# One loop, seven trips of two batches in place of fourteen trips of one

## The chip, the cores and the metric

The kernel runs on one core of a Trainium2 chip. The core has five engines that run at once, each with an instruction stream of its own: TensorE (PE: matrix products and transposes), VectorE (DVE), ScalarE (ACT), GpSimd (POOL) and SyncE (SP, which here only issues DMAs). In front of each engine a sequencer reads the stream, works out register values, waits for semaphores, branches, and hands the real work to its engine. In the profile, a name with a q at its end (ACTq, DVEq, PEldq) is such a sequencer. The metric is the time of one execution on the device in microseconds (us), lower is better; three runs of the kernel before gave 1945.77, 1946.47 and 1946.70 us.

## The reference, cut to what matters

Each of 16 batches (512 tokens of width 256) goes through a normalisation, an attention branch of 16 heads with a feed-forward part, and a gated branch whose operands are rounded to a 4 bit grid; the two are multiplied and added to the input:

```python
x = L0_attn_x                                  # (16, 512, 256)
xn = _layernorm(x, axis=-1)
s = _L0_attn_ref(xn, ...)                      # attention, layernorm, gelu feed-forward, layernorm
g = _silu(_L0_ffn_ref(xn, w_gate, w_up, w_down))
x = x + s * g
```

## The kernel before, in words

All work is written out by hand as named steps, one ordered list for each engine (`ORDER`). There are three parts. The part `head` prepares weights and handles the first batch, the part `end` handles the last one, and the part `mid` is the steady state. One pass through `mid` is one batch, but it is a software pipeline: it takes the attention scores of batch b, the output side (`cT`, `out`, `hT`, `f1`, `f2`) of batch b-1 and the input side (`xT`, `proj`, `v`) of batch b+1.

The five engines meet only through semaphores that count up over the whole kernel and are never reset. `Event.wait` (L68) turns a batch number into the count to wait for: `b * (per * by) + (k + 1) * by`. Where b is known, that is a constant; in the loop b is a register, and the sequencer works the count out (ALU_OP and FUSED_REGOPS records of L68) just ahead of the instruction that waits for it.

`program` (L1630 to L1634) puts the parts together for one engine: the head once, then a loop of fourteen trips over `mid` with the trip's register as the batch number, then the end. Each engine has its own loop and its own branch back; there is no barrier at the end of a trip. At this seam the engines do the following, and the steps of the prediction are here:

- TensorE ends its list with `ctxt.3 mT.0 dn.3` (L716 is `dn`) and begins it with `cT` (L723: eight transposes of the finished attention context) and `out.0 out.1` (L731: the output projection).
- ScalarE ends with `mT.0 dn.3` (L812, L878) and begins with `cT` (L889: copies the transposed context to `catT`, which `out` reads).
- VectorE ends with `mfin.0 ctxt.3 dn.3` (L1125 is `dn`) and begins with `out.0 out.1` (L1133: adds the projection to `hY`), then `ln1`.
- SyncE ends with `fin mio.0` and begins with `T.0 load.1`: loads of the tables `Tz` (L552) and of `KS` and `QS` (L527).
- GpSimd ends with `hr.3` and begins with `ln1`, which waits for VectorE.

So in the order of the data the seam is: `dn.3` on TensorE, `cT` on TensorE, `cT` on ScalarE, `out` on TensorE, `out` on VectorE.

Of the kernel before, what the change touches and what calls it, by code (L numbers as in the profile page):

```python
# [15 lines left out]
B, S, D = 16, 512, 256  # L16
# [40 lines left out]
class Event:  # L57
# [5 lines left out]
    def wait(self, eng, b, k=None):  # L63

        if isinstance(b, int) and b < 0:
# [96 lines left out]
    mid=dict(  # L162
        sync="""
            T.0 load.1 T.1 T.2 xload T.3 mio.1 T.4 splitio T.5 load.0 T.6 T.7 fin mio.0
        """,
        gpsimd="""
            ln1 mul.0 lnb1 xnb mul.1 hq.0 mul.2 hr.0 projm.0 mul.3 hq.1 projm.1 hr.1 projm.2 xq xr mul.4 hq.2 mul.5
            ln2 hr.2 fin mul.6 hq.3 mul.7 hr.3
        """,
        vector="""  # L170
# [140 lines left out]
def build(nc, x_d, w, out_d):  # L311
    with ExitStack() as ctx:
# [1316 lines left out]

        def program(steps, eng):  # L1630
            steps(eng, "head", PARTS["head"])
            with eng.Fori(1, B - 1) as b:
                steps(eng, "mid", dict(mid=b))
            steps(eng, "end", PARTS["end"])  # L1634

        with nc.Block() as block:
            @block.sync
            def _(sp):
                program(sync_steps, sp)
                d_out.wait(sp, B - 1, 1)  # L1640

            @block.gpsimd
            def _(pool):
                program(gpsimd_steps, pool)

            @block.vector
            def _(dve):
                program(vector_steps, dve)

            @block.tensor  # L1650
            def _(pe):
                program(tensor_steps, pe)

            @block.scalar
            def _(act):
                program(scalar_steps, act)
# [33 lines left out]
```

How the kernel before makes its waits and increments, by code:

```python
    def wait(self, eng, b, k=None):  # L63
        if isinstance(b, int) and b < 0:
            return
        k = self.per - 1 if k is None else k
        eng.wait_ge(self.sem, b * (self.per * self.by) + (k + 1) * self.by)
# [350 lines left out]
        def inc(ins, name):  # L419
            ins.then_inc(E[name].sem, 1)
# [56 lines left out]
        def sync_steps(sp, part, at_batch):  # L477
# [27 lines left out]
                        cols, r = slice(t * P, (t + 1) * P), 2 * H * t  # L505
                        sp.dma_start(qb_d[:, 3:6, cols], bias_sp[r:r + H]).then_inc(d_split.sem, 16)
                        sp.dma_start(kb_d[:, 0:3, cols], bias_sp[r + H:r + 2 * H]).then_inc(d_split.sem, 16)
                elif k == "load":
                    half = s[1]
                    hb = half_batch(half, b)
                    if which != "pro":
                        E["pe_sc"].wait(sp, hb - 1, 24 * half + 23)
                    if which == "pro":
                        sp.wait_ge(L["ready"], 3)
                        sp.wait_ge(L["ones"], 32)
                    d_split.wait(sp, hb)
                    pairs = slice(HALF * half, HALF * (half + 1))
# [24 lines left out]
                        E["g_mul"].wait(sp, b, p - 2)  # L543
                    else:
                        v_mul[1].wait(sp, b - 1, PAIRS - 2 + p)
                        E["g_mul"].wait(sp, b - 1, PAIRS - 2 + p)
                    if which == "first" and p < 2:
                        sp.wait_ge(L["rows"], 16 * 5)
                    for e in range(2):
                        r = rows_d[b, 2 * p + e, :]
```

## Time and profile before

| | us |
|---|---|
| median of three runs (lowest to highest) | 1946.47 (1945.77 to 1946.70) |
| profiled execution, its time | 1947.52 |
| its span, first to last instruction | 1945.70 |
| TensorE busy (matrix products) | 1820.7 (94%) |
| VectorE busy | 1615.3 (83%) |
| GpSimd busy | 1103.7 (57%) |
| ScalarE busy | 901.9 (46%) |

The head takes the first 252 us, the fourteen trips go from there to 1801 us, and the end takes the rest. Register, branch and semaphore instructions are not counted as busy; a view of one source line lists them with their start. L1632 is the line of the loop: its records are the move and the first register work of a trip, and at the trip's end the addition and the compare-and-branch. The profile also lists the DMA queues; queues of the kind "instruction" carry the instruction stream itself to the sequencers.

### The profile page before, as it was taken

The page shows a single profiled execution, that of the slowest core. Times are in us where ns is not written, and L with a number is a line of the kernel's source. Part 1 is how long each engine was busy: PE and PEld are TensorE (multiplying, and loading weights), DVE is VectorE, ACT ScalarE, POOL GpSimd, SP SyncE. Part 2 cuts the span into 40 slices and gives each one's busy share as a digit, 9 for nine tenths or more (in the row PEclk, how much of TensorE's full clock was granted, in tenths as well). Part 3 has the DMA queues.
Part 4 walks back from the last instruction along what each step waited for, and adds up shares of the span by engine and source line. Part 5 has one row for each costly group of instructions (what it writes and reads, how often), then busy time and mean ns, then how long its engine had stood idle before and what let it go on. Part 6 is the DMA issues. An engine that isn't in the chain of part 4 may idle for free.

```text
span 1945.7 us, 42571 instructions
## 1 busy us (share of the span) xinstructions
PE 1820.7 (94%) x12700; PEld 1311.4 (67%) x12700; DVE 1615.3 (83%) x5197; ACT 901.9 (46%) x1833; POOL 1103.7 (57%) x799
## 2 busy tenths in 40 slices
PE   8667999999999999999999999999999999999997
PEld 3234677676776767677776767677676767677766
DVE  7868879888898988888997988888897988889763
ACT  3024454454635445453545445463545445363542
POOL 3434746565664746465674756466574656566563
PEclk8777999999999999999999999999999999999999
DMA  5343223232223333232322323222332323322211
GB/s 170 117 123 89 64 74 108 65 105 73 77 74 83 108 73 95 65 103 70 93 76 73 107 75 95 73 82 71 99 90 73 107 62 103 77 78 74 63 56 33
DMA packets 138566, 165.35 MB, mean 85 GB/s; under 512 B 19758, under 2 KB 100655, under 8 KB 138453
## 3 DMA queue, kind: packets, MB, share of 16 engines
q1 hardware_dynamic: 138458, 164.30, 30.5%
q14 instruction: 87, 0.70, 0.1%
q8 instruction: 21, 0.34, 0.1%
HBM read 127.85 MB, written 36.41 MB: 84 GB/s over the span
## 4 chain that ended last, share of the span: by engine, by line
PE 60%; DVE 15%; issue 12%; POOL 6%; ACT 3%; DMA 3%; SPq 1%; DVEq 0%; ACTq 0%; POOLq 0%
PE ps L767 11%; PE ps L758 11%; PE ps L699 8%; PE ps L716 4%; PE ps L622 3%; PE ps L609 3%; PE ps L656 3%; PE ps L595 3%; POOL Pr L1174 3%; PE ps L672 2%; PE ps L731 2%; PE ps L652 2%; DVE st L956 2%; DVE nmax L1035 2%; DMA QS<-q_bias_parts 2%
## 5 line engine op out<-in xcount | busy, mean ns | idle before, releaser
L1174 POOL TENSOR_TENSOR Pr<-Pr,Tz 128x768 f32<-128x768 f32 (+2 forms) x384 | 478.2, 1275 | 248.5 <-ACT Pr L831 244.6
L1035 DVE CUSTOM_DVE_ANT_0 ps<-ps,future 128x512 f32<-128x512 f32 (+3 forms) x1024 | 474.6, 516 | 51.2 <-issue 50.9
L831 ACT ACTIVATE Pr<-ps 128x384 f32<-128x384 f32 x512 | 243.8, 489 | 352.7 <-PE ps L656 348.6
L622 PE MATMUL ps<-KS,QS 108*128 108x512 bf16 (+3 forms) x1024 | 218.3, 304 | 32.5 <-DVE nmax L1035 23.9
L758 PE MATMUL ps<-catT,w 128*128 128x256 f32 x1024 | 237.8, 380 | 0.7 <-ACT catT L894 0.7
L767 PE MATMUL ps<-w,gT 128*128 128x256 f32 x1024 | 232.9, 381 | 0.9 <-ACT gT L911 0.9
L1065 DVE SCALAR_TENSOR_TENSOR Pr<-ps,Tz 128x512 f32<-128x512 f32 x256 | 175.2, 684 | 54.7 <-ACT ps L820 46.7
L820 ACT ACTIVATE ps<-ps 128x512 f32<-128x512 f32 x256 | 150.4, 588 | 139.9 <-PE ps L652 138.4
L767 PEld LDWEIGHTS ps<-w,gT 128*128 128x128 f32 x1024 | 190.8, 190 | 25.7 <-ACT gT L911 1.3
L758 PEld LDWEIGHTS ps<-catT,w 128*128 128x128 f32 x1024 | 189.6, 190 | 26.3 <-ACT catT L894 0.9
L716 PE MATMUL ps<-wdT,hqT 128*128 128x256 f32 x768 | 178.0, 381 | 0.7 <-ACT hqT L870 0.7
L656 PE MATMUL ps<-QS,KS 112*128 112x384 bf16 (+2 forms) x768 | 162.7, 276 | 16.1 <-DVE Pr L1065 11.7
L699 PE MATMUL ps<-wgT,xqT 128*128 128x352 f32 x512 | 176.0, 466 | 0.2 <-ACT xqT L851 0.2
L699 PE MATMUL ps<-wuT,xqT 128*128 128x352 f32 x512 | 172.4, 459 | 0.0
L1213 POOL TENSOR_TENSOR slot<-slot 128x704 f32<-128x704 f32 x64 | 107.6, 1681 | 97.5 <-DVE slot L939 97.5
L622 PEld LDWEIGHTS ps<-KS,QS 108*128 108x128 bf16 x1024 | 88.2, 98 | 106.7 <-DVE nmax L1035 48.5
L1223 POOL TENSOR_TENSOR rstd<-ve,minus_half 128x4 f32<-128x4 f32 (+1 forms) x34 | 33.4, 982 | 223.4 <-DVE ve L964 222.0
L716 PEld LDWEIGHTS ps<-wdT,hqT 128*128 128x128 f32 x768 | 142.4, 190 | 20.1 <-ACT hqT L870 1.1
L672 PE MATMUL ps<-Pr,v_cur 128*17 128x128 f32 (+2 forms) x3584 | 152.5, 321 | 0.6 <-ACT hqT L870 0.6
L1035 DVE DVE_READ_ACCUMULATOR2_ANT nmax<- 128x1 f32 x1024 | 142.7, 139 | 0.0
L699 PEld LDWEIGHTS ps<-wuT,xqT 128*128 128x128 f32 x512 | 97.2, 190 | 54.4 <-ACT ctxT L846 0.3
L672 PEld LDWEIGHTS ps<-Pr,v_cur 128*17 128x17 f32 x3584 | 95.2, 98 | 53.2 <-issue 40.8
(226 smaller groups left out, 3252.0 us busy)
## 6 DMA issues: line engine op xcount, KB each, us to landing
Tz<-kernel_rows SPq DMA_DIRECT2D x256, 256.0 KB, 3.5
KS<-k_parts SPq DMA_DIRECT2D x32, 384.0 KB
QS<-q_parts SPq DMA_DIRECT2D x64, 192.0 KB
hY<-in_x SPq DMA_DIRECT2D x19, 512.0 KB, 4.8
xn<-in_x SPq DMA_DIRECT2D x17, 512.0 KB, 3.5
out<-y SPq DMA_DIRECT2D x15, 512.0 KB, 3.0
q_parts<-q_sp SPq DMA_DIRECT2D x16, 384.0 KB, 3.1
k_parts<-k_sp SPq DMA_DIRECT2D x16, 384.0 KB, 2.4
```

Of the source, the lines that this page charges most:

```text
L622: ins = mm(o, QS[0:KROWS, 2 * p + e, it * P:(it + 1) * P], KS[0:KROWS, p, 0:n], start=True, stop=True)
L656: ins = mm(dst[:, at:at + PAST[j]], KS[0:SROWS, p, j * P:(j + 1) * P], rhs[:, S - 1:P * (j + 1) - 1:-1], start=True, stop=True)
L672: ins = mm(dst[32 * hh:32 * hh + HD + 1, to:to + n], v_cur[:, j, 4 * g + hh, :], rhs[:, n - 1::-1], start=i == 0, stop=i == len(pieces) - 1)
L699: ins = mm(dst[:, 0:IH], xqT[:, c, t * P:(t + 1) * P], wt[:, c, f * IH:(f + 1) * IH], start=c == 0, stop=c == KD - 1)
L716: ins = mm(dst[:, 0:D], hqT[:, c * P:(c + 1) * P], wdT[:, c, :], start=c == 0, stop=c == KI - 1)
L758: ins = mm(dst[:, i * n:(i + 1) * n], w1[:, c, f * P:(f + 1) * P], catT[:, c, hf * n:(hf + 1) * n], start=c == 0, stop=c == KD - 1)
L767: ins = mm(dst[:, 0:D], gT[:, f, at:at + P], w2[:, f, :], start=f == 0, stop=f == KF - 1)
L820: inc(af(src, src, ACT.Exp), "a_exp")
L831: inc(af(Pr[:, p % 4, e, at:at + wd], src[:, 0:wd], ACT.Exp), "a_exp")
L1035: ins = v.tensor_tensor_reduce(o, o, future[:, S - n:S], -1.0, 3e38, ALU.add, ALU.min, nmax[:, 2 * pl + e, it:it + 1])
L1065: v.scalar_tensor_tensor(blocks(Pr[:, p % 4, e, 0:S]), blocks(ps[:, SC_BANKS[n % len(SC_BANKS)], :]), 3e38, near, ALU.min, ALU.mult).then_ ...
L1174: ins = g.tensor_tensor(a, a, Tz[:, p % 2, :, P * j:P * j + PAST[j]], ALU.mult)
```

## The change

The loop runs over seven trips, and its body holds the steps of `mid` twice, once for each of two batches. The batch numbers are 2 x trip + 1 and 2 x trip + 2, computed from the trip's register. The order of steps within a batch, the semaphores, the buffers and every engine instruction stay as they are. All five engines get the same form of loop.

```diff
         def program(steps, eng):
             steps(eng, "head", PARTS["head"])
-            with eng.Fori(1, B - 1) as b:
-                steps(eng, "mid", dict(mid=b))
+            with eng.Fori(0, (B - 2) // 2) as trip:
+                for second in range(2):
+                    steps(eng, "mid", dict(mid=trip * 2 + (1 + second)))
             steps(eng, "end", PARTS["end"])
```

## Rows read from the trace of the kernel before

**Rows 1.** The page, part 4: the chain that ended last, share by engine.
```profile
PE 60%; DVE 15%; issue 12%; POOL 6%; ACT 3%; DMA 3%; SPq 1%; DVEq 0%; ACTq 0%; POOLq 0%
```
**Rows 2.** Busy time by stretch: stretch, length, engines (xinstructions), clock, DMA, GB/s.
```profile
473.60:584.00 110.40, 107.17 (x777) 79.26 (x776) 95.09 (x305) 54.36 (x110) 65.43 (x47) 1.00 0.30 84
...
363.00:1801.00 1438.00, 1395.24 (x10090) 1032.44 (x10089) 1234.12 (x3965) 706.91 (x1430) 850.53 (x611) 1.00 0.31 84
```
**Rows 3.** Timeline of the second seam: start, duration, engine, line, operation [idle before <-releaser].
```profile
473.73 1.04 PE L723 MATMUL ps<-ident,ctxn 128*128 128x128 f32 x8
473.93 0.39 ACT L878 ACTIVATE dth<-ps 128x256 f32<-128x256 f32 x1 [2.20 <-PE ps L716]
...
474.54 1.08 ACT L889 ACTIVATE catT<-ps 128x512 f32<-128x512 f32 x2 [0.22 <-PE ps L723]
...
475.67 3.72 PE L731 MATMUL ps<-ow,catT 128*128 128x256 f32 x16 [0.91 <-ACT catT L889]
...
477.70 0.69 DVE L1133 TENSOR_TENSOR hY<-ps,xnb 128x512 f32<-128x512 f32 x1 [2.94 <-PE ps L731]
```
**Rows 4.** Timeline where the loop is entered without a branch back.
```profile
254.59 3.72 PE L731 MATMUL ps<-ow,catT 128*128 128x256 f32 x16 [0.92 <-ACT catT L889]
...
256.62 0.69 DVE L1133 TENSOR_TENSOR hY<-ps,xnb 128x512 f32<-128x512 f32 x1 [2.95 <-PE ps L731]
```
**Rows 5.** Line L1632: duration ns min/median/max, first to last start; second seam, then whole run.
```profile
L1632 ACTq COMPARE_BRANCH  x1: 45/45/45, 474.0 to 474.0; - x1
L1632 ACTq FUSED_REGOPS  x1: 59/59/59, 474.3 to 474.3; - x1
...
L1632 DVEq COMPARE_BRANCH  x1: 68/68/68, 474.4 to 474.4; - x1
...
L1632 DVEq FUSED_REGOPS  x1: 74/74/74, 477.4 to 477.4; - x1
...
L1632 PEldq COMPARE_BRANCH  x14: 83/215/243, 360.6 to 1798.6; - x14
```
**Rows 6.** Line L68 (the waits' register work) over one trip, 473.60 to 584.04.
```profile
L68 DVEq ALU_OP  x99: 40/40/40, 477.7 to 580.6; - x99
L68 ACTq ALU_OP  x77: 35/35/35, 474.6 to 575.2; - x77
L68 ACTq EVENT_SEMAPHORE  x40: 17/17/38, 474.6 to 581.7; - x40
L68 DVEq EVENT_SEMAPHORE  x38: 21/21/689, 477.5 to 580.9; - x38
```
**Rows 7.** DMA queues (packets, MB, share): 252 to 363; 473.5 to 584; 363 to 1801.
```profile
q8 instruction: 6, 0.10, 0.4%
q14 instruction: 7, 0.06, 0.2%
...
q14 instruction: 5, 0.04, 0.1%
...
q14 instruction: 65, 0.53, 0.1%
```
**Rows 8.** Busy time of TensorE in short stretches, with the granted clock.
```profile
175.60:178.80 3.20, 1.73 (x11) 1.00 0.98 331
179.00:192.40 13.40, 11.37 (x42) 0.50 0.45 138
...
196.00:199.30 3.30, 3.27 (x33) 0.50 0.03 7
...
704.60:707.80 3.20, 1.54 (x11) 1.00 0.78 157
```
**Rows 9.** Groups by line, 185.7 to 192.5 us and 480 to 560 us.
```profile
L609 PE MATMUL ps<-vw,xnT 128*128 128x256 f32 x8 | 3.7, 643 | 0.4 <-DVE nmax L1035 0.4
...
L609 PE MATMUL ps<-vw,xnT 128*128 128x256 f32 x16 | 3.8, 382 | 0.0
```
**Rows 10.** Waits (us in total, times, longest), 363 to 1790 us.
```profile
PE ps L622 <- DMA QS<-q_bias_parts: 4.8, 7, 1.7
```

## The prediction

> **What bounds the kernel now.** The page comes first. The chain that ended last lies on TensorE for 60% of its length and on VectorE for 15% [rows 1]. The table of busy time by stretch says the same of the loop: in a trip of 110.4 us TensorE is busy 107.2 us, VectorE 95.1, GpSimd 65.4 and ScalarE 54.4, and over the thirteen trips from 363 to 1801 us the granted clock is 1.00, its upper level of 2.4 GHz [rows 2]. So whatever holds TensorE up inside the loop is lost, and 3 us a trip at most are free. Since the change touches no engine instruction, I read the seam between two trips next, in the timeline: TensorE transposes from 473.73, ScalarE copies from 474.54, TensorE starts the projection at 475.67, VectorE takes its first half at 477.70 [rows 3]. TensorE already stands idle for 0.91 us here, waiting for ScalarE's copy, so a delay of ScalarE at the seam is a delay of TensorE. Third, the records of the loop's own line [rows 5], and last the queues that carry instructions [rows 7].
>
> **What a branch back costs today.** The reader is to see two kinds of branch in [rows 5]. ScalarE's starts at 474.0, and the first record of the next trip starts at 474.3: 0.3 us. VectorE's starts at 474.4, and the next record starts only at 477.4: 2.9 us after the branch ended. In those 2.9 us the sequencer has nothing to hand over. The instruction queues name the reason: in every trip five packets of q14 arrive (5 in one trip, 65 in thirteen), of 0.53 MB / 65 = 8 KB each [rows 7]. One engine's stream is read anew in every trip, and the others are not. TensorE's stream comes on q8 in packets of 0.10 / 6 = 16 KB; six arrive in the first trip, and in the thirteen others that queue isn't listed at all. So TensorE's body, and ScalarE's, which branch at once, stay in their sequencers, and VectorE's doesn't.
>
> How long are the bodies? A trip has 110 ScalarE instructions [rows 2] and 77 + 40 of register and semaphore work [rows 6], with some 17 more 244 in all. VectorE has 305 + 99 + 38, with some 20 more about 460. So on these engines 244 instructions stay and 460 don't. TensorE has 777 products and 776 weight loads [rows 2] and some 155 others, about 1710, and these stay.
>
> VectorE's gap is free today. Its `out.0` waits for the projection anyway: 2.03 us after the projection's start, at the seam with a branch (475.67 to 477.70, [rows 3]) as at the entry without one (254.59 to 256.62, [rows 4]).
>
> **The change part by part.**
>
> Removed: seven of thirteen taken branches (fourteen trips have thirteen, seven have six). On ScalarE, SyncE, GpSimd and TensorE a branch takes 0.2 to 0.3 us, and TensorE's sequencer is 2.6 us ahead of its array there (branch at 360.6, transposes of that seam at 363.2, which is 473.7 less one trip). On VectorE the 2.9 us are hidden, as shown. So the gain is 0.
>
> Added: register work for 2 x trip + 1. A record of it lasts 35 to 74 ns [rows 5, 6]; two or three more a batch on each engine, beside running work, are nothing, and if all were on the path, 14 x 0.1 = 1.4 us. I take 0.
>
> Doubled: the bodies. ScalarE's becomes 488 instructions, more than the 460 of VectorE that don't stay. It uses packets of the same size and the same queue, since no other instruction queue is listed. So I expect ScalarE to get VectorE's kind of branch at the six seams that still have one. Its next record then comes 2.9 us after the branch in place of 0.2: 2.7 us later. Ahead of the copy it has register work up to about 474.5 and starts at 474.54, so nothing covers these 2.7 us, and the copy starts at 477.2. The transposes it needs are done long before. The projection starts 2.7 us later, at 478.4, and everybody in the chain waits for that: VectorE, whose own gap is covered more than before, GpSimd behind VectorE's statistics, and TensorE itself, whose list is in order, so that the scores and the gate products behind `out` stand too. 6 x 2.7 = +16.2 us.
>
> TensorE's body becomes about 3420 instructions. The trace shows only that 1710 stay. If 3420 don't, the price is VectorE's gap and a larger packet: q8 took 0.4% x 16 x 111 / 6 = 1.2 us each and q14 0.1% x 16 x 110.5 / 5 = 0.35 [rows 7], so 2.9 + 0.85 = 3.7 us, 3.5 more than now. The sequencer has a lead of 2.6 us, of which register work and the branch take some 0.8, so the transposes would come 1.7 us late, at 475.4, and be done by 476.5. That is inside ScalarE's delay, which ends at 477.2. Its cost beside ScalarE's is 0; alone it would be 6 x 1.7 = 10.2 us.
>
> SyncE and GpSimd: GpSimd's doubled body (47 engine instructions a trip, [rows 2]) stays well under 244 instructions. SyncE's lies near 244; if it missed, its first loads of a trip would come 2.7 us later, together with everything that uses them. 0.
>
> Inside the doubled body the stream is read in order. VectorE does that today, and TensorE in the first trip, whose length doesn't differ from the others'. 0, and at most a few tenths each.
>
> Given back: at the seam SyncE starts loads of `QS` and `KS` which TensorE sometimes waits for, 4.8 us over thirteen trips [rows 10]. With TensorE 2.7 us later these waits vanish at six seams: 4.8 x 6 / 13 = -2.2 us, bounds 0 and -2.2; I take -2.0.
>
> The clock. After the change TensorE would stand idle from 473.9 to 475.4, work for 1.0 us, and stand idle to 478.4. The rows show what such stretches do. Between 175.6 and 178.8 TensorE was busy 1.73 of 3.2 us at clock 1.00, and from 179.0 the clock was 0.50, the lower level of 1.2 GHz. With 1.54 of 3.2 us busy at 704.6 it held [rows 8]. The seam after the change, with 1.0 us of work between two idle stretches of 1.5 and 1.9 us, is sparser than both, so I expect the clock to fall at most of the six seams. The price: eight products of L609 took 3.7 us at the lower level, and sixteen took 3.8 at the upper one [rows 9], so work takes double. A fall lasted 13.4 us at 179.0, where work was thin, and 3.3 us at 196.0, where TensorE was full [rows 8]. Behind the seam it is full. So 3.3 / 2 = 1.65 us are lost at most for a short one, part of which falls into the idle time; I take 1.4. Bounds: 0, and two short ones in a row, 3.3. 6 x 1.4 = +8.4 us.
>
> Sum: 16.2 - 2.0 + 8.4 = +22.6 us. The profiled span becomes 1945.7 + 22.6 = 1968.3, the profiled execution 1947.5 + 22.6 = 1970.1. The median lies 1.05 us under the profiled execution: 1969.1 us.
>
> **The skill's capacity.** VectorE's 460 instructions are read anew in each trip [rows 6, 7]. The Trainium skill says otherwise: "Runtime: NRT & Kernel Launch", Instruction fetch mechanics, gives most engines 512 instructions and TensorE 2048, and says that a taken branch to a page that isn't there forces a fetch. By its capacity VectorE's 460 and ScalarE's 488 would both fit, and TensorE's 3420 would not: that is the second rival. For VectorE the trace disagrees, so its figure is doubtful for ScalarE too; for TensorE nothing here tests it.
>
> **The rivals.**
>
> 1. ScalarE misses, but the clock holds. For it: the clock held at 704.6, in a stretch that looks much like the one at 175.6, and it never fell at a seam so far. Then 16.2 - 2.0 = +14.2: 1960.7 us.
> 2. Only TensorE misses, and ScalarE's 488 instructions stay. For it: the row on VectorE doesn't say where between 244 and 460 the line lies, nor that both engines have the same one. 10.2 us, and a fallen clock at a seam or two, +2: 1958.7 us. It decides from a body over what TensorE holds.
> 3. Nothing misses that matters, and the time is not slower: if ScalarE and TensorE hold their doubled bodies (TensorE's limit is unseen, and ScalarE could hold more than VectorE), six short branches replace thirteen, all beside other work: 1946.5 us. It decides at one point, whether ScalarE's first record of a trip comes 0.2 or 2.9 us after its branch. That it would be faster needs a seam where VectorE's gap ends last; the two rows I compare show 2.03 us both times.
> 4. The misses are longer. Three sequencers fetch within a few us while SyncE's loads begin, and the clock stays low for two spells: 6 x (3.3 + 3.0) - 2 = +36: 1982 us.
>
> **How the numbers follow.** The forecast gets 0.50, rival 1 0.20, rival 2 0.10, rival 3 0.09, rival 4 0.09, and some gain that I don't see 0.02. The range reaches from rival 2 to just short of rival 4, 1956 to 1981 us, which holds 0.80. A measurement of this kernel can tell about 0.2%, 3.9 us, from no change. Slower by more than that: 0.50 + 0.20 + 0.10 + 0.09 = 0.89; within it: 0.09; faster: 0.02.
>
> **What would show it.** In the records of L1632, ScalarE's gap from branch to next record is 2.9 us at six seams, and VectorE's stays; q14 brings about seven packets a batch in place of five, and q8 brings TensorE's body in each trip, some 12 to 14 packets of 16 KB. In the timeline the idle time of ScalarE ahead of L889 grows to about 3 us at every second seam, and TensorE's ahead of L731 with it, while seams inside a trip look as now. The granted clock shows short spells of 0.50 behind those seams. The sum is wrong if ScalarE's gap stays at 0.2 us, if TensorE's transposes come later than 477 us on the clock of the second seam, or if the time between two seams inside a trip grows too, which would mean that reading in order isn't free.

## The result, and the profile after

The changed kernel takes 1969.0 us (median of four executions, 1966.6 to 1978.1, so they scatter by 11.5) where the kernel before takes 1946.3 beside it (1945.8 to 1946.7): a ratio of 1.0122, with a 95% interval of 1.0104 to 1.0141. It is slower by 22.7 us. The profiled execution took 1966.63 us, with a span of 1964.8.

The page's parts 1, 3 and 4 come first (busy us with share and instruction count; queues with packets, MB and share; the chain by engine).

```profile
PE 1824.1 (93%) x12700; PEld 1314.3 (67%) x12700; DVE 1612.7 (82%) x5197; ACT 900.8 (46%) x1833; POOL 1103.1 (56%) x799
...
q8 instruction: 118, 1.93, 0.4%
q14 instruction: 113, 0.92, 0.2%
...
PE 60%; DVE 18%; issue 13%; POOL 4%; ACT 3%; DMA 2%; DVEq 1%; SPq 0%; ACTq 0%; POOLq 0%
```

The engines did the same work: the same counts, and busy times within 4 us of those of before. Only the instruction queues stand out. From 363 to 1801 us, about thirteen batches, the view of the queues has:

```profile
q8 instruction: 96, 1.57, 0.5%
q14 instruction: 89, 0.73, 0.2%
```

q8, with TensorE's packets of 16 KB, wasn't listed in the loop before and now brings 96; q14 brings 89 where it brought 65 [rows 7]. Two bodies that used to stay are now read anew. The records of the loop's line say what that costs. First the whole run (duration in ns as min/median/max, first to last start), then the seam of the second branch back alone:

```profile
L1632 PEldq COMPARE_BRANCH  x7: 83/3385/3624, 468.0 to 1817.7; - x7
...
L1632 PEldq COMPARE_BRANCH  x1: 3322/3322/3322, 691.5 to 691.5; - x1
L1632 ACTq COMPARE_BRANCH  x1: 45/45/45, 694.3 to 694.3; - x1
...
L1632 DVEq COMPARE_BRANCH  x1: 68/68/68, 694.7 to 694.7; - x1
...
L1632 ACTq FUSED_REGOPS  x1: 59/59/59, 697.4 to 697.4; - x1
L1632 DVEq FUSED_REGOPS  x1: 74/74/74, 697.9 to 697.9; - x1
```

ScalarE branches at 694.3, and its next record is at 697.4: 3.1 us, where it was 0.3 [rows 5]. VectorE keeps its gap of some 3 us. TensorE's wait lies inside the record of its branch, whose median went from 215 ns [rows 5] to 3385. The timeline of the same seam answers to [rows 3]:

```profile
694.21 0.38 ACT L878 ACTIVATE dth<-ps 128x256 f32<-128x256 f32 x1 [2.25 <-PE ps L716]
...
695.10 1.09 PE L723 MATMUL ps<-ident,ctxn 128*128 128x128 f32 x8 [0.93 <-issue]
...
697.68 1.09 ACT L889 ACTIVATE catT<-ps 128x512 f32<-128x512 f32 x2 [3.09 <-issue]
...
698.82 5.20 PE L731 MATMUL ps<-ow,catT 128*128 128x256 f32 x16 [2.63 <-ACT catT L889]
...
702.49 0.69 DVE L1133 TENSOR_TENSOR hY<-ps,xnb 128x512 f32<-128x512 f32 x1 [7.44 <-PE ps L731]
```

Before, the copy of catT started 0.61 us after the copy of dth (473.93 to 474.54, [rows 3]). Here it starts 3.47 after it (694.21 to 697.68), so it is 2.86 late. The transposes came after an idle time of 0.93 and were long done. "<-issue" at the copy says that ScalarE waited for nothing but its own instructions. And the sixteen products of L731 took 5.20 us where they took 3.72. The busy times by stretch show why (length, the five engines, the granted clock, DMA share, GB/s):

```profile
698.40:701.80 3.40, 2.98 (x7) 2.44 (x8) 0.00 (x0) 0.37 (x1) 0.00 (x0) 0.50 0.94 241
...
471.80:475.20 3.40, 1.57 (x10) 1.31 (x11) 0.00 (x0) 1.08 (x2) 0.00 (x0) 1.00 0.24 60
```

Behind this seam the clock was granted at 0.50, its lower level of 1.2 GHz, for 3.4 us. The same stands behind the seams at 923.7, 1149.0, 1374.3 and 1599.5. At the first seam, at 471.8, it stayed at 1.00, the upper level of 2.4 GHz:

```profile
471.82 1.09 PE L723 MATMUL ps<-ident,ctxn 128*128 128x128 f32 x8 [1.08 <-issue]
...
473.58 1.08 ACT L889 ACTIVATE catT<-ps 128x512 f32<-128x512 f32 x2 [2.42 <-PE ps L723]
...
474.72 3.50 PE L731 MATMUL ps<-ow,catT 128*128 128x256 f32 x15 [1.81 <-ACT catT L889]
```

There the copy was 2.2 us late and TensorE idle for 1.08 us ahead of the transposes and 1.81 ahead of the projection, not 0.93 and 2.63. But the seam at 1370 looks the same, with the copy 2.1 us late, and there the clock fell (the fence shows three of the sixteen products, which took 5.41 us together):

```profile
1370.99 1.09 PE L723 MATMUL ps<-ident,ctxn 128*128 128x128 f32 x8 [0.96 <-issue]
...
1373.96 1.38 PE L731 MATMUL ps<-ow,catT 128*128 128x256 f32 x3 [1.88 <-ACT catT L889]
```

So the length of the idle time alone doesn't tell whether the clock falls; what else decides is open.

**The sum over the loop.** The loop's length can be read from the last copy of dth ahead of its entry to that ahead of its exit. The first fence is the kernel before, the second the changed one:

```profile
252.84 0.38 ACT L878 ACTIVATE dth<-ps 128x256 f32<-128x256 f32 x1 [2.26 <-PE ps L716]
...
1801.34 0.38 ACT L878 ACTIVATE dth<-ps 128x256 f32<-128x256 f32 x1 [2.20 <-PE ps L716]
```

```profile
249.57 0.38 ACT L878 ACTIVATE dth<-ps 128x256 f32<-128x256 f32 x1 [2.26 <-PE ps L716]
...
1820.44 0.38 ACT L878 ACTIVATE dth<-ps 128x256 f32<-128x256 f32 x1 [2.25 <-PE ps L716]
```

It went from 1548.50 to 1570.87 us: +22.4. The copy of catT was late by 2.19, 2.86, 2.61, 2.52, 2.14 and 2.91 us at the six seams, 15.2 together. Behind the five with the lower clock the sixteen products of L731 took 5.20, 5.19, 5.41, 5.41 and 5.41 us where they took 3.72, 8.0 more together. Batch by batch, from one last copy of dth to the next, the six behind a branch back took 112.8 to 115.2 us in place of 110.55, 23.3 more, which is these two terms. At the seven seams inside a trip the copy follows dth after 0.44 us instead of 0.61, but their batches took 110.1 to 110.7 us, and only 0.2 less together. And the loop of before holds one batch of 111.33 us, 0.8 over its others. In it TensorE waits 1.66 us for a load of QS:

```profile
707.72 0.61 PE L622 MATMUL ps<-KS,QS 108*128 108x512 bf16 x3 [1.66 <-DMA QS<-q_bias_parts]
```

That batch has no counterpart after the change, so 23.3 - 0.2 - 0.8 = 22.3 of the 22.4. The span grew by 19.1 only, since the head of this execution was 3.3 us shorter (249.57 against 252.84); the head isn't touched by the change and ended between 247.7 and 255.3 us in the runs below.

### The profile page after: what moved, and what is told of

It reads as the page before. It is cut to its first block, busy times and chain, and to the rows that moved or that the text cites. A ratio compares the mean times of both kernels' runs of the same rounds, so it can differ in the third digit from the quotient of the medians.

```text
span 1964.8 us, 42305 instructions
## 1 busy us (share of the span) xinstructions
PE 1824.1 (93%) x12700; PEld 1314.3 (67%) x12700; DVE 1612.7 (82%) x5197; ACT 900.8 (46%) x1833; POOL 1103.1 (56%) x799
## 4 chain that ended last, share of the span: by engine, by line
PE 60%; DVE 18%; issue 13%; POOL 4%; ACT 3%; DMA 2%; DVEq 1%; SPq 0%; ACTq 0%; POOLq 0%
PE ps L767 11%; PE ps L758 11%; PE ps L699 8%; PE ps L716 4%; PE ps L731 3%; PE ps L622 3%; PE ps L656 3%; PE ps L609 3%; PE ps L595 3%; PE ps L672 2%; PE ps L652 2%; DVE st L956 2%; DVE nmax L1035 2%; DVE ps L1035 1%; POOL Pr L1174 1%
## 5 line engine op out<-in xcount | busy, mean ns | idle before, releaser
L1065 DVE SCALAR_TENSOR_TENSOR Pr<-ps,Tz 128x512 f32<-128x512 f32 x256 | 175.8, 687 | 54.7 <-ACT ps L820 47.8
```

The costliest lines, as they stand in the source:

```text
L1065: v.scalar_tensor_tensor(blocks(Pr[:, p % 4, e, 0:S]), blocks(ps[:, SC_BANKS[n % len(SC_BANKS)], :]), 3e38, near, ALU.min, ALU.mult).then_ ...
```

## The experiments

The theory is the prediction's: a body that its sequencer doesn't hold is read anew after each branch back, ScalarE's delay is TensorE's delay, and the clock falls behind it. The rivals are that TensorE's own reading is what costs, that the new register work or the branch itself is what costs, and that the clock's fall comes of the reading and not of the idle time. "Period" below is the time from one copy of dth (`dn.3`) to the next, 110.55 us in the loop before.

### One engine at a time

The loop is written so that some engines get seven trips of two batches and the others keep fourteen of one. This works because they meet only through counts.

```diff
-            with eng.Fori(1, B - 1) as b:
-                steps(eng, "mid", dict(mid=b))
+            if steps in (scalar_steps,):
+                with eng.Fori(0, (B - 2) // 2) as trip:
+                    for second in range(2):
+                        steps(eng, "mid", dict(mid=trip * 2 + (1 + second)))
+            else:
+                with eng.Fori(1, B - 1) as b:
+                    steps(eng, "mid", dict(mid=b))
```

The tuple names the engines: ScalarE here, TensorE in the second run, the other three in the third.

> Only ScalarE's loop has seven trips of two batches; the other four engines keep fourteen trips of one. Theory A (ScalarE's stream is fetched anew behind its branch, and that stall with the clock that falls behind it is the whole loss): at six seams ScalarE's copy starts 2.2 to 2.9 us late, in sum about 15 us, and the clock falls behind most of them, 1.5 us each: 1946.3 + 22 = 1968 us, as much as the full change. Theory B (TensorE's longer body is what costs): 1946 us. Theory C (both add up): halfway, about 1960 us.

ScalarE alone: 1965.3 us, 1.0100 times before (1.0074 to 1.0127). The timeline at its first branch back:

```profile
471.57 1.09 ACT L889 ACTIVATE catT<-ps 128x512 f32<-128x512 f32 x2 [2.66 <-issue]
...
472.71 5.41 PE L731 MATMUL ps<-ow,catT 128*128 128x256 f32 x16 [3.34 <-ACT catT L889]
```

The copy was 2.2 to 2.5 us late at six seams, 14.1 together, TensorE's transposes were in time, and the clock stood at 0.50 for 3.4 us behind five of the six. At the sixth, at 921.0, TensorE was idle for 3.12 us and the clock held; that batch grew by 2.2 us, where those with a fall grew by 3.9 to 4.2. So most of the price is there with ScalarE's doubled body alone.

> Only TensorE's loop has seven trips of two batches. Theory A: TensorE's own fetch comes late by 3.4 us less its lead; its transposes start 1.4 us late at six seams, and without ScalarE's stall beside it the projection does too: 6 x 1.4 = 8.4 us, the clock holds, 1955 us. The part is hidden in the full change behind ScalarE's stall. Theory B (TensorE's body is the whole loss): 1968 us. Theory D (the trace's late transposes cost nothing even alone): 1946 us.

TensorE alone: 1955.95 us, 1.0052 (1.0035 to 1.0070). The timeline at two of its branches back:

```profile
694.03 1.09 PE L723 MATMUL ps<-ident,ctxn 128*128 128x128 f32 x8 [1.02 <-issue]
...
696.02 3.72 PE L731 MATMUL ps<-ow,catT 128*128 128x256 f32 x16 [0.91 <-ACT catT L889]
...
916.70 1.09 PE L723 MATMUL ps<-ident,ctxn 128*128 128x128 f32 x8 [1.26 <-issue]
...
918.70 5.41 PE L731 MATMUL ps<-ow,catT 128*128 128x256 f32 x16 [0.91 <-ACT catT L889]
```

The transposes are 1.0 to 1.7 us late, and the copy 1.1 to 1.7, 8.3 over six seams. The clock fell behind two of them (5.41 in place of 3.72), 3.4 us: 11.7, and the loop grew by 11.6 (from 1548.5 to 1560.1). It fell here with no more than 1.26 and 0.91 us of idle time at 918.7, and held at 1141 with 1.50 and 0.91. The two prices don't add up: +18.9 (1965.3 - 1946.4) and +9.6 alone, +22.7 together. TensorE's 1.5 us lie inside ScalarE's 2.5.

> VectorE's, GpSimd's and SyncE's loops have seven trips of two batches, ScalarE's and TensorE's fourteen of one. Theory A: VectorE keeps its gap of 2.9 us at six seams, hidden as before, and loses it at seven; GpSimd and SyncE stay with short branches: 1946 us, at best 0.5 us less. Theory E (the three add to the loss, through later loads or a later VectorE): 1949 us or more.

VectorE, GpSimd and SyncE: 1949.85 us, 1.0010 (0.9995 to 1.0024). Its periods alternate between 110.57 and 110.95 us, so a trip of two batches costs 0.4 us, 2 to 3 us over the whole loop. Behind a branch back the projection's first half is taken 2.18 us after its start, instead of 2.03, but that batch keeps its 110.57. The longer one is the trip's second batch. In it, 81 us behind the seam inside the trip, TensorE waits 0.69 us for VectorE's Pr (L1065), where it waited 0.1 before; why VectorE is late there is open.

### No branch at all

```diff
-            with eng.Fori(1, B - 1) as b:
+            for b in range(1, B - 1):
                 steps(eng, "mid", dict(mid=b))
```

> No loop at all: the fourteen batches of the middle stand one behind the other on every engine, and batch numbers are constants, so the register work is gone too. Theory A (a stream that is read in order costs nothing, only a branch to code that is no longer there does): no stall at any seam, 1946 us or up to 2 us less, since VectorE's gap and the register work are gone. Theory F (reading streams longer than what a sequencer holds costs in itself): 1950 us or more, spread over the batches.

1941.1 us, 0.9965 (0.9947 to 0.9983), with a period of 109.83 us. All streams are read in order throughout, and the periods show no stall of the size of a missed branch (109.8 to 109.9 us, one of 110.4). That beats both kernels, by 5.2 us at the median, though 0.7 us a batch would be 14 x 0.7 = 10. Part of it goes in the end part, where the clock fell for 3.4 us in its profiled execution; its ten executions lay between 1933.5 and 1944.8.

### Is it the reading?

The changed kernel, with a hint of the coming branch for three sequencers:

```diff
-            with eng.Fori(0, (B - 2) // 2) as trip:
+            hinted = steps in (scalar_steps, tensor_steps, vector_steps)
+            with nc.Fori(0, (B - 2) // 2, engines=OrderedEngineSet([eng.engine]), hint_back_edge=hinted) as trip:
```

1950.6 us, 1.0031 (1.0013 to 1.0048): 17.6 of the 22.7 us are gone. The records of the loop's line, TensorE's branches of the whole run and ScalarE's at the first branch back:

```profile
L1634 PEldq COMPARE_BRANCH  x7: 87/360/392, 467.3 to 1795.3; - x7
...
L1634 ACTq COMPARE_BRANCH  x1: 68/68/68, 470.1 to 470.1; - x1
L1634 ACTq BRANCH_PREFETCH_HINT  x1: 31/31/31, 470.3 to 470.3; - x1
```

And the timeline of the first branch back:

```profile
469.81 1.04 PE L724 MATMUL ps<-ident,ctxn 128*128 128x128 f32 x8
470.01 0.38 ACT L879 ACTIVATE dth<-ps 128x256 f32<-128x256 f32 x1 [2.26 <-PE ps L717]
...
470.65 1.09 ACT L890 ACTIVATE catT<-ps 128x512 f32<-128x512 f32 x2 [0.26 <-PE ps L724]
...
471.79 3.72 PE L732 MATMUL ps<-ow,catT 128*128 128x256 f32 x16 [0.94 <-ACT catT L890]
```

ScalarE's gap is 0.2 us again at all six seams, VectorE's is 0.5, and TensorE's branch takes 360 ns. The hint's record stands at the top of a trip, so it comes a whole trip, some 220 us, ahead of the branch that it tells of. And fewer packets come on q14: the page has 77 where the changed kernel's has 113 (q8: 113 for 118). So the loop's head is there when the branch comes; whether the hint brings it in time or keeps it from being replaced, this run doesn't tell. From the first copy of dth to the last the loop took 1548.8 us, as before, though TensorE waits more for the loads of QS: 11.3 us at ten places from 363 to 1790 us, against 4.8 at seven. The batches with such a wait of 1.1 us or more took 110.8 to 111.3 us, the others 110.1 to 110.6. What is left lies behind the loop: the last period, which ends in the end part, took 110.7 us where it took 105.9. At the exit ScalarE's copy came 2.2 us late, which fits a sequencer that has the loop's head ready and then has to go on (a guess: no other run tests it), and further on the clock fell for 3.4 us.

```profile
1798.02 0.38 ACT L879 ACTIVATE dth<-ps 128x256 f32<-128x256 f32 x1 [2.26 <-PE ps L717]
...
1800.62 1.08 ACT L890 ACTIVATE catT<-ps 128x512 f32<-128x512 f32 x2 [2.21 <-issue]
```

The same bodies, branches and register work, with one hint a trip, cost next to nothing in the loop: this rules out the register work and the branch as such.

### How much does ScalarE hold?

The kernel before, with empty instructions in ScalarE's body, 160 in one run and 100 in the other:

```diff
                 k = s[0]
+                if which == "mid" and k != "cT" and padded < 160:
+                    for _ in range(4):
+                        act.nop("pad", nofuse=True)
+                        padded += 1
```

> The kernel before, with its fourteen trips of one batch and its register work, and 160 empty instructions (nops) for ScalarE's sequencer spread over its trip behind cT, four ahead of each step: its body grows from 244 to 404 instructions, and nothing else changes. ScalarE has 56 us of a trip idle, so the nops themselves cost little. Theory A (what counts is the body's length): 404 is more than ScalarE holds, ScalarE's gap behind the branch becomes some 2.6 us at all thirteen seams, the copy is late each time, the clock falls at most of them, and the time grows by 13 x (2.5 + 0.8 x 1.5) = 48 us: 1994 us, 1980 to 2000. If 404 is still held: 1946 to 1950 us with a gap of 0.2 us. Theory B (the changed kernel's gap comes of its new register work, 2 x trip + 1, behind the branch): 1946 to 1950 us as well, so a result near 1994 falls it.

> As the run with 160 nops, with 100: a body of 344 instructions on ScalarE. Theory A with a store of four blocks of 128 instructions, of which one is for the block that comes next in order: the loop's first instruction lies some 30 places into a block, so 344 instructions touch three blocks, which stay beside the next one; ScalarE's gap stays near 0.2 us and the time at 1946 to 1950 us. With 404 they touch four, which don't. If the limit lies below 344, the gap becomes some 2.6 us here too, and the time 1980 to 2000 us.

With 160 (a body of 404 instructions) it took 2003.4 us, 1.0292 (1.0275 to 1.0309). With 100 (344 instructions) it took 1944.2 in one execution, and its periods are 110.57 us but for one of 111.38, in which TensorE waits 1.7 us for QS. A nop lasts 14 ns, so 160 are 2.2 us of ScalarE's 56 idle ones. The timelines of the two at their third branch back, 160 first:

```profile
591.95 0.39 ACT L883 ACTIVATE dth<-ps 128x256 f32<-128x256 f32 x1 [2.20 <-PE ps L716]
...
595.01 1.08 ACT L894 ACTIVATE catT<-ps 128x512 f32<-128x512 f32 x2 [2.68 <-issue]
...
596.15 6.72 PE L731 MATMUL ps<-ow,catT 128*128 128x256 f32 x16 [3.37 <-ACT catT L894]
```

```profile
580.93 0.38 ACT L883 ACTIVATE dth<-ps 128x256 f32<-128x256 f32 x1 [2.20 <-PE ps L716]
...
581.54 1.08 ACT L894 ACTIVATE catT<-ps 128x512 f32<-128x512 f32 x2 [0.23 <-PE ps L723]
```

ScalarE's gap behind the branch is 2.4 to 2.7 us at all thirteen seams with 404 instructions, and 0.2 with 344; q14 brings 128 packets from 363 to 1801 us with 404, and the 65 of before with 344. Here the loop, its register work and its trips are those of the kernel before. So what counts is the body's length, and ScalarE's limit for a loop at this place in the code lies between 344 and 404. I had put 48 us on it, and it cost 58. TensorE's waits for the copy grew from 11.8 to 41.6 us over thirteen seams, 29.8, where I had put 32; the lower clock stood behind every seam, for 3.4 us at ten (some 1.6 lost each) and for 6.8 us at three, as at 596.15 (6.72 - 3.72 = 3.0 lost), 25 us where I had put 16. The idle times don't tell the two kinds apart: 3.37 us came ahead of a short one at 367 and of a long one at 596.

The Trainium skill, "Runtime: NRT & Kernel Launch", Instruction fetch mechanics, gives 512 instructions for these engines, 2048 for TensorE, and a block of 16 KiB for 256 instructions. TensorE agrees: 1710 stay and the 3409 of the changed kernel don't. ScalarE's 404 don't, against 512. The packets of q8 are of 16 KB, as the page has it, but those of q14 are of 8 KB, which makes 128 instructions by the page's figures. As an estimate from them, the store would be four such blocks; a body that starts some 30 places into a block touches three with 344 instructions and four with 404, and the store holds the loop only if the block that is brought ahead of its end has room too. That fits VectorE's 460 and both runs here, but it isn't shown: no run shows the blocks, and the 30 places are assumed (from 41 places on, 344 instructions would touch four blocks as well).

### The stall without the reading

The kernel before, with 4 (and in another run 1) more copies on ScalarE ahead of cT in each trip, into a buffer that nobody reads:

```diff
+                    if which == "mid":
+                        for i in range(4):
+                            if i:
+                                E["a_rest"].wait(act, b - 1, i - 1)
+                            inc(af(rest[:], future[:], ACT.Copy), "a_rest")
+                        E["a_rest"].wait(act, b - 1, 4 - 1)
                     for c in range(KD):
                         E["pe_cT"].wait(act, b - 1, c)
```

> The kernel before, with its loop and with streams that are held as before; ahead of cT in each of the fourteen trips ScalarE makes four more copies of 128x512 into a buffer that nobody reads, each waiting for the one before. By the copies of catT (1.08 us for two) they take 2.2 to 3 us, so cT on ScalarE comes 2 to 2.8 us late at all fourteen seams, as behind a missed branch, but nothing is fetched. Theory A (of the changed kernel's price some 2.5 us a seam are ScalarE's lateness and some 1.5 a fallen clock where TensorE idles that long): 14 x 2.4 = 34 and 9 to 14 falls x 1.5 = 14 to 21: 1994 to 2001 us, with stretches of clock 0.50 of 3.4 us behind most seams. Rival (the clock's fall has to do with the fetching, not with the idle time): clock 1.00 throughout the loop, 1977 to 1984 us.

2020.3 us, 1.0382 (1.0365 to 1.0399), more than either theory gave. The timeline of its second branch back:

```profile
481.36 2.62 ACT L890 ACTIVATE rest<-future 128x512 f32<-128x512 bf16 x4
...
484.26 1.09 ACT L897 ACTIVATE catT<-ps 128x512 f32<-128x512 f32 x2 [0.28 <-ACT rest L890]
...
485.40 6.40 PE L731 MATMUL ps<-ow,catT 128*128 128x256 f32 x16 [3.61 <-ACT catT L897]
```

And the busy times of two stretches behind it:

```profile
484.00:487.40 3.40, 2.00 (x5) 1.65 (x6) 0.00 (x0) 1.09 (x2) 0.00 (x0) 0.51 0.94 239
487.50:490.90 3.40, 3.40 (x9) 2.68 (x9) 0.69 (x1) 0.00 (x0) 0.00 (x0) 0.51 1.12 229
```

TensorE idles 3.61 - 0.91 = 2.70 us longer, and its products take 6.40 - 3.72 = 2.68 longer: 5.4 us, by which this trip grew (115.95 against 110.55; later ones took 116.05). ScalarE's gap is 0.2 throughout, and q14 brings no more than VectorE's packets (63 from 363 to 1801 us). So the clock falls behind a stall without any more reading, and the rival that it has to do with the reading is out. Here it was already down when the products began and stayed down for 6.8 us at thirteen seams, where I had counted on 3.4; that is the miss of my sum.

> The kernel before, with one more copy of 128x512 by ScalarE ahead of cT in each trip, into a buffer that nobody reads. By e8_delay4's group of four (2.62 us) it takes 0.65 us, and with the wait for it the copy of catT comes some 0.6 us late at all fourteen seams; nothing is fetched. Theory A (lateness of ScalarE passes one to one into the time while TensorE's clock stays up): the clock holds in the loop, each trip is 0.6 us longer, 14 x 0.6 = 8.4: 1954 to 1956 us. If the clock falls at such a short stall too: 14 x (0.6 + 1.5) = 29, 1975 us. If part of the lateness is taken up by slack behind the seam: under 1951 us.

1956.2 us in one execution; theory A gave 1954 to 1956. The timeline of a branch back:

```profile
586.21 0.63 ACT L890 ACTIVATE rest<-future 128x512 f32<-128x512 bf16 x1
...
587.14 1.08 ACT L897 ACTIVATE catT<-ps 128x512 f32<-128x512 f32 x2 [0.30 <-ACT rest L890]
588.27 3.07 PE L731 MATMUL ps<-ow,catT 128*128 128x256 f32 x13 [1.63 <-ACT catT L897]
```

And the busy times over the loop, with the clock in the third column from the end:

```profile
363.00:1800.00 1437.00, 1385.86 (x9989) 1024.37 (x9988) 1225.67 (x3937) 711.38 (x1436) 847.02 (x609) 1.00 0.31 84
```

TensorE idles 1.63 - 0.91 = 0.72 us longer, the clock holds over the whole loop, and the period is 111.28, longer by 0.73. A late copy at the seam passes one to one into the time. The waits of TensorE for the loads of QS [rows 10] are no longer listed in this run. What that gives back is the 0.8 us of the one longer batch of before and no more: the loop grew by 9.4 us (from 1548.5 to 1557.9), and 14 x 0.73 - 0.8 = 9.4.

### Where the loop without branches gains

SyncE, TensorE or VectorE alone written out, the others in the loop of before:

```diff
+            if steps in (vector_steps,):
+                for b in range(1, B - 1):
+                    steps(eng, "mid", dict(mid=b))
+            else:
                 with eng.Fori(1, B - 1) as b:
                     steps(eng, "mid", dict(mid=b))
```

> The kernel before, with SyncE alone written out without a loop, its batch numbers constants; the others keep their fourteen trips. Written out everywhere, a batch took 109.83 us instead of 110.55. Where does that 0.7 come from? Theory S (SyncE's loads of KS and QS go out sooner when no register work stands ahead of their waits, and TensorE waits for these loads): periods of 110.0 to 110.3 us here. Theory T (TensorE's own register work at the seam): 110.55 as before. Time 1939 to 1943 or 1946 us.

> The kernel before, with TensorE alone written out without a loop, its batch numbers constants. Theory T (TensorE's register work and branch hold it up): a period of 109.9 to 110.2 us in place of 110.55, 1937 to 1942 us. Theory S or V (it is SyncE's or VectorE's): 110.55, 1946 us. The stream is then read in order throughout, in packets of 16 KB, at no cost by the kernel that is written out everywhere.

> The kernel before, with VectorE alone written out without a loop, its batch numbers constants: its gap of 2.9 us behind the branch goes and so does its register work. Theory V (VectorE's register work stands between its operations, whose ends release TensorE): a period of 109.9 to 110.3 us in place of 110.55, 1937 to 1943 us. If VectorE's gap and register work are covered, as the prediction has it: 110.55, 1946 us.

The periods are 110.56 us with SyncE, 110.53 with TensorE and 110.27 with VectorE written out (single executions of 1946.6, 1950.7 and 1941.6 us; the middle one has a longer head, with the first copy of dth at 255.3 us, and a low clock in the end part). So theories S and T fall, and VectorE's register work and gap are worth 0.28 us a batch. At a seam without a branch ScalarE's copy follows 0.44 us after dth instead of 0.61, 0.17 less. The run with ScalarE alone doubled has such seams inside its trips, and the batches behind six of the seven lasted 110.24 to 110.27 us, 0.28 less than 110.55. If ScalarE's 0.28 and VectorE's 0.28 add up, which no run tests, some 0.16 of the 0.72 are not located.

## Why the prediction was right

**The seam decides.** It said that what holds TensorE up at the seam is lost. The run with one added copy shows it: 0.72 us of idle time, 0.73 us of period.

**Removed branches, register work: 0.** Near enough in sum: the seven batches behind a seam inside a trip are 0.2 us shorter together. But two terms that I hadn't listed seem to hide in it: with ScalarE alone doubled these batches are some 0.28 us shorter each, and with VectorE, GpSimd and SyncE doubled they are some 0.4 longer each.

**ScalarE's body: 16.2.** The mechanism is shown by the runs with ScalarE alone, with the hint and with the nops. The size was 15.2, 2.5 us a seam for 2.7: ScalarE's gap was 2.4 to 3.1 us, at four of six seams under VectorE's 2.9. (Its body has 475 records from branch to branch, not 488; both are over the 404 that don't stay.)

**TensorE's body: late by 1.7, hidden, 10.2 alone.** Its transposes were late by 1.1 to 1.4 us and lay inside ScalarE's delay. Alone it costs 9.6 us by the medians. By its profiled loop it costs 11.6, of which 8.3 are lateness, 1.4 a seam for 1.7, and 3.4 are the clock, which I had left out of the 10.2 and put at 2 in rival 2. The gap of TensorE's sequencer, 3.3 to 3.6 us, is near the estimate of 3.7.

**Given back: -2.0. This step was mis-sized.** The waits for QS went down as expected, from 4.8 us [rows 10] to 1.1:

```profile
PE ps L731 <- ACT catT L889: 17.8, 12, 2.7
...
PE ps L622 <- DMA QS<-q_bias_parts: 1.1, 3, 0.6
```

But only 0.8 us came back, the one longer batch of before. I could have seen it: the waits fall on seven of thirteen trips, and six of those seven lasted 110.5 to 110.6 us like the trips without. Only the wait of 1.66 us at 707.72 lengthened its trip, to 111.33, and by 0.8. The waits of up to 0.8 us cost nothing, so they had nothing to give back.

**The clock: 8.4.** It was 8.0: five seams of six, at 1.5 to 1.7 us, where I had six at 1.4. The short fall of 3.3 us came as read from [rows 8]. That two stretches in a row are possible, one of my bounds, the runs with four copies and with 160 nops show.

**The sum.** +22.6 was forecast and +22.4 measured in the loop. The errors cancel: 1.2 too much given back, against 1.0 too much for ScalarE and 0.4 for the clock. The agreement to a tenth or two is luck, and so is that of the medians (1969.1 and 1969.0), since four executions scatter by 11.5 us and the profiled one took 1966.6 for the 1970.1 forecast, its head being 3.3 us shorter. The terms are right to about 1 us. Of the signs I named, the gap, the idle time at every second seam and the short low clock came as told; q14 brought 89 packets in 13 batches, 6.8 each for "about seven"; q8 brought 96, 15 a trip for "12 to 14".

**The rivals.** The clock didn't hold (rival 1). TensorE alone would have given 1956.0 (rival 2: 1958.7), but ScalarE missed too. Rival 3 is what the hint nearly makes of it. Rival 4, misses of 3.3 us with two stretches of low clock behind every seam, didn't come: the copy was 2.5 us late on average, and each of the five falls lasted 3.4 us. 6.8 us stood behind every seam of the loop only with four copies added and TensorE idle for 3.6 us.

## What to carry to other kernels

Fewer trips of a longer body is not a saving when the branches lie beside other work: what counts is whether each engine's body still fits into its sequencer, and whether something covers the first 3 us after the branch on that engine (here nothing did on ScalarE, and the projection's 2.03 us and more did on VectorE). The profile tells much of it before the change is made: packets of an instruction queue in the steady state tell that a body doesn't fit, and the time from the branch's record to the next tells the price. It didn't tell where between 244 and 460 instructions ScalarE's limit lies; the runs with nops did, in part. If a long body is wanted, give the loop a branch hint or, where the code's size allows it, write it out.

## What the runs showed that I had not expected

- ScalarE held a loop of 344 instructions and not one of 404; where the body isn't held, the first record comes 2.4 to 3.1 us after the branch on ScalarE and 2.7 to 3.2 on VectorE, and TensorE's branch, with packets of 16 KB, lasts 3.3 to 3.9.
- With a hint for the branch 2.4 to 3.1 us became 0.2 on ScalarE, 2.9 became 0.5 on VectorE, and 3.4 became 0.36 on TensorE, though the hint stands a whole trip ahead of its branch. The same run has a late start at the exit, 2.2 us once on ScalarE.
- Idle time has a second price. 0.7 us more of it at the seam cost 0.7; 2.4 mostly cost 4.1 (2.4 and a clock of 0.50 for 3.4 us); 2.7 cost 5.4, with the clock low for 6.8 us. The length of the idle time alone doesn't decide: with ScalarE alone 2.2 us more at 921.0 cost 2.2, and with TensorE alone the clock fell behind 1.26 and 0.91 us of idle time and held behind 1.50 and 0.91.
- Instructions read in order cost nothing that shows: the kernel without a loop, whose streams are never held, has the shortest period, 109.83 us. (The 0.4 us a trip with VectorE, GpSimd and SyncE doubled are not explained.)
- Most waits for a load cost nothing: of those for QS in the loop before, only one of 1.66 us lengthened its trip.
